# A two-layer graph kernel: first tiles of columns 3 to 6 taken through both hops inside column 1

## The chip, the cores and the metric

The kernel runs on one core of a Trainium2 chip. The metric is the device time of one execution in microseconds (us), the median of several runs. The engines are named as the profile names them: PE is TensorE (PEld its weight loads), DVE is VectorE, ACT is ScalarE, POOL is GpSimd, SP the engine that issues the large loads.

## The reference

The graph has 8192 nodes with 128 features each, and `adj` is a symmetric 8192 x 8192 float32 matrix of zeros and ones (256 MB). Three products with it are computed, each followed by a small projection:

```python
h = maximum(layernorm(x), 0)
x1 = swish((adj @ h) @ W0 + b0)          # first hop
x = x + swish((adj @ x1) @ W0 + b0)      # second hop
h = maximum(layernorm(x), 0)
a_hat = adj + eye;  d = sum(a_hat, axis=1) ** -0.5
out = ((a_hat * d[:, None] * d[None, :]) @ h) @ W1.T + b1   # third hop
x = x + out
```

## The kernel before

**Work and tiles.** The output nodes are split into 16 columns of 512. A tile is 512 source nodes by one column, 1 MB in float32, so that a column has 16 tiles and `adj` has 256. Each tile is loaded once, into a ring of 4 buffers (`ring`, `RING`). DVE or ACT turns it into one byte per element (`mark`, `act_mark`; the tiles in `ACT_MARKED` are ACT's), in a ring of 8 byte tiles (`marks`, `MARK_RING`), and DVE packs four byte tiles at a time to one bit per element (`pack_half`, `pack_again`, `pack_last`), which is kept in `bits` for later. A buffer of `ring` is free for the next load when its tile is marked and, unless the tile is in `LATE`, when ACT has also counted its nonzero elements with a Sign activation (`counted`). SP waits for just that before each load. A tile in `LATE` is loaded again in the third hop and counted there.

**The first hop** multiplies every tile with h: 8 matmuls of 512 columns for each tile, in order of arrival, into `acc_ps`. When column c is done, its sums go through a chain over four engines: ACT `sums_out`, PE `project`, DVE `add_bias` and `scale_z`, ACT `sigmoid`, DVE `gate`, ACT `high_part`, DVE `low_part`. The last sets `node_ready`: the result of column c is then an input of the second hop. `FINISH` and `FINISH_FIRST` give the tile of the next column behind which each of these steps stands.

**The second hop, as far as it can be done while tiles arrive.** Tile i of column c needs the first hop's result of column i alone. In column c the tiles up to c - 2 are therefore multiplied a second time at once (`early`, into `early_ps`), and for columns 0 to 2 the missing blocks are unpacked from `bits` (`kept_unpack`) and multiplied a little later (`kept_block`, 12 blocks of two matmuls in a column, 8 the first time). `AHEAD` puts tiles of late columns into the order of the earlier ones: behind tiles 7 and 11 of columns 2 and 3, two columns at a time, the first two tiles of each. Such a tile is taken through both hops on the spot (`unit_ahead`), the partial sums are moved out by ACT (`save_x` after the first hop's 16 matmuls, `save_y` after the second's), and POOL adds them back when the column's own turn comes. The tiles' own places are then holes.

**After the last load**, `PIECES` goes through the rest of the second hop and the whole third hop from `bits`, unpacked by DVE into `ring` in pieces of two units (`unpack`), four pieces ahead of PE at most. In the third hop each column is a step k of 64 blocks (128 matmuls) and one projection; in each, SP loads `LATE_STEP` tiles of `LATE` again, and ACT (Sign) and DVE (`late_check`) count them. All engines run their instructions in the order of the program, so that whatever waits holds up what is behind it on its engine.

## Time and profile before

| | us |
|---|---|
| runs | 1430.45, 1431.73, 1432.16 (median 1431.73) |
| profiled execution, its own time | 1429.92 |
| its span, first to last instruction | 1428.1 |
| PE busy | 1382.2 (97%) |
| DVE busy | 1055.0 (74%) |
| ACT busy | 685.2 (48%) |

A timeline row gives the start and the length of an instruction in us, engine, line, what it writes and reads, and in brackets how long the engine had been idle before it and who ended that. The length of a matmul in such a row (0.38) overlaps with the next one's; the distance between two starts is what one costs. The tiles are numbered below by the order in which they are loaded, from 0: "load 16" is tile 0 of column 1.

### The profile page before, as it was taken

The numbers are of one execution on the slowest core, as the hardware profiler recorded it, in microseconds if no ns is written. First come the engines' busy times: TensorE is split into PE (matmuls) and PEld (weight loads), VectorE is DVE, ScalarE is ACT, GpSimd is POOL, SyncE is SP. The second block draws the span as 40 slices with busy tenths as digits, with TensorE's granted clock in tenths as the row PEclk, the third lists the DMA queues.
The fourth block names the chain that finished last, engine by engine and source line by source line (L and its number), as shares of the span: only waits on it lengthen the run. The fifth ranks groups of instructions, "written<-read, shape, count | busy, mean of one in ns | idle before, by whom it ended". The sixth has DMA issues, their size and how long they took to land.

```text
span 1428.1 us, 18554 instructions
## 1 busy us (share of the span) xinstructions
PE 1382.2 (97%) x6600; PEld 650.5 (46%) x6600; DVE 1055.0 (74%) x2327; ACT 685.2 (48%) x798; POOL 62.1 (4%) x47
## 2 busy tenths in 40 slices
PE   3889999999999999999999999999999999999997
PEld 1334444444444444444444454454444444444443
DVE  7878777899999988977694767786766566657630
ACT  6785738888878676567540122222322322332200
POOL 1100000000100100000000011100000000000000
PEclk9999999999999999999999999999999999999999
DMA  9999999999999988798730112112453435343300
GB/s 395 409 421 394 406 405 385 413 421 414 400 392 395 367 346 323 308 370 320 315 150 30 52 45 68 66 67 89 192 195 144 191 134 198 141 190 136 139 23 17
DMA packets 58420, 352.23 MB, mean 247 GB/s; under 512 B 6481, under 2 KB 6866, under 8 KB 18386
## 3 DMA queue, kind: packets, MB, share of 16 engines
q1 hardware_dynamic: 51696, 339.11, 59.6%
q10 hardware_dynamic: 6626, 11.87, 2.2%
q8 instruction: 55, 0.90, 0.3%
q14 instruction: 43, 0.35, 0.1%
HBM read 339.15 MB, written 11.80 MB: 246 GB/s over the span
## 4 chain that ended last, share of the span: by engine, by line
PE 87%; DMA 6%; ACT 3%; DVE 2%; issue 1%; SPq 0%; POOL 0%; ACTq 0%; DVEq 0%
PE acc_ps L740 21%; PE acc_ps L741 21%; PE acc_ps L675 11%; PE acc_ps L676 11%; DMA ring<-adj 6%; PE early_ps L606 5%; PE early_ps L604 5%; PE z_ps L587 3%; PE kept_ps L614 2%; PE kept_ps L615 2%; ACT marks L816 1%; PE acc_ps L631 1%; PE early_ps L645 1%; PE acc_ps L632 1%; PE early_ps L644 1%
## 5 line engine op out<-in xcount | busy, mean ns | idle before, releaser
L899 ACT ACTIVATE unused<-ring 128x2048 uint8<-128x2048 uint32 x204 | 389.4, 1909 | 70.5 <-DMA ring<-adj 61.5
L675 PE MATMUL acc_ps<-marks,node_a 128*128 128x512 fp8e4 x960 | 368.0, 383 | 35.3 <-DVE node_a L1057 24.6
L741 PE MATMUL acc_ps<-ring,node_a 128*128 128x512 fp8e4 x1024 | 388.1, 379 | 0.0
L740 PE MATMUL acc_ps<-ring,node_a 128*128 128x512 fp8e4 x1024 | 388.1, 379 | 0.0
L676 PE MATMUL acc_ps<-marks,node_a 128*128 128x512 fp8e4 x960 | 368.0, 383 | 0.0
L1065 DVE TENSOR_SCALAR marks<-ring 128x2048 uint8<-128x2048 f32 x230 | 285.6, 1242 | 81.1 <-DMA ring<-adj 40.0
L1354 DVE TENSOR_SCALAR_CACHE_REDUCE count_a<-marks 128x2048 uint8<-128x2048 f32 x52 | 118.7, 2284 | 113.9 <-DMA marks<-adj 112.5
L437 DVE TENSOR_SCALAR ring<-bits 128x256 uint32<-128x256 uint32 (+1 forms) x784 | 158.7, 276 | 40.7 <-PE acc_ps L741 40.5
L675 PEld LDWEIGHTS acc_ps<-marks,node_a 128*128 128x128 f16 x960 | 94.7, 99 | 156.8 <-issue 48.5
L741 PE MATMUL acc_ps<-ring,node_b 128*128 128x512 fp8e5 x416 | 157.7, 379 | 0.0
L740 PE MATMUL acc_ps<-ring,node_b 128*128 128x512 fp8e4 x416 | 157.7, 379 | 0.0
L740 PEld LDWEIGHTS acc_ps<-ring,node_a 128*128 128x128 f16 x1024 | 100.3, 98 | 118.8
L741 PEld LDWEIGHTS acc_ps<-ring,node_a 128*128 128x128 f16 x1024 | 100.2, 98 | 119.0
L676 PEld LDWEIGHTS acc_ps<-marks,node_a 128*128 128x128 f16 x960 | 94.7, 99 | 113.2 <-issue 4.6
L947 ACT ACTIVATE nT<-acc_ps 128x512 f32<-128x512 f32 x16 | 9.6, 597 | 264.4 <-PE acc_ps L741 264.4
L604 PE MATMUL early_ps<-marks,node_b 128*128 128x512 fp8e4 x352 | 133.4, 379 | 0.0
L606 PE MATMUL early_ps<-marks,node_b 128*128 128x512 fp8e5 x352 | 133.4, 379 | 0.0
L955 ACT ACTIVATE unused<-marks 128x2048 uint8<-128x2048 uint32 x52 | 99.2, 1908 | 56.5 <-DMA marks<-adj 54.9
L1073 DVE SCALAR_TENSOR_TENSOR xnew<-marks 128x1024 uint32<-128x1024 uint32 (+1 forms) x68 | 81.8, 1203 | 0.4 <-ACT marks L816 0.4
L932 ACT ACTIVATE y<-xnew,nmr,rstd 128x128 f32<-128x128 f32 x64 | 26.4, 483 | 104.3 <-DVE nmr L1347 104.3
L1157 DVE TENSOR_TENSOR zb<-z_ps,b_sb 128x512 f32<-128x512 f32 x32 | 22.1, 690 | 62.9 <-PE z_ps L587 62.7
L614 PE MATMUL kept_ps<-kept_marks,node_b 128*128 128x512 fp8e4 x164 | 62.1, 379 | 1.7 <-issue 1.7
(137 smaller groups left out, 1205.8 us busy)
## 6 DMA issues: line engine op xcount, KB each, us to landing
ring<-adj SPq DMA_DIRECT2D x256, 1024.0 KB, 7.8
marks<-adj SPq DMA_DIRECT2D x52, 1024.0 KB, 5.4
node_b<-x SPq DMA_DIRECT2D x4, 1024.0 KB, 11.0
xch<-x SPq DMA_DIRECT2D x16, 256.0 KB, 2.8
xn_scratch<-xnew ACTq DMA_DIRECT2D x16, 256.0 KB, 2.0
xch<-xn_scratch SPq DMA_DIRECT2D x16, 256.0 KB, 2.8
out<-xnew ACTq DMA_DIRECT2D x16, 256.0 KB, 2.0
part_scratch<-stage ACTq DMA_DIRECT2D x13, 256.0 KB, 7.0
```

The source lines that it names most:

```text
L437: return nc.vector.tensor_scalar(dst, src, abs(MARK_BIT - BIT[k]), MARK_WORD, shift, ALU.bitwise_and)
L604: nc.tensor.matmul(into[:, :], hi_of(node_b16, j), byte.bitcast(E4), start=(j == (2 * TB if c in AHEAD_COLUMNS else 0)), stop=False)
L606: last = nc.tensor.matmul(into[:, :], lo_of(node_b16, j), byte.bitcast(E5), start=False, stop=(c > 2 and j == (c - 1) * CB - 1))
L614: nc.tensor.matmul(kept_ps[n][:, :], hi_of(node_b16, j), byte.bitcast(E4), start=(j == 0), stop=False)
L675: nc.tensor.matmul(acc_ps[c % 2][:, :], hi_of(node_a16, j), byte, start=(j == opens * TB), stop=False)
L676: last = nc.tensor.matmul(acc_ps[c % 2][:, :], lo_of(node_a16, j), byte, start=False, stop=(j == NB - 1))
L740: nc.tensor.matmul(into[:, :], hi_of(node, j), byte.bitcast(E4), start=opens, stop=False)
L741: last = nc.tensor.matmul(into[:, :], lo_of(node, j), byte.bitcast(low), start=False, stop=closes)
L899: nc.scalar.activation(unused[:, :], loaded_slot(g).bitcast(U32), ACT.Sign, accum_out=nz_count[:, g:g + 1]).then_inc(counted, 1)
L955: nc.scalar.activation(unused[:, :], late_slot(e).bitcast(U32), ACT.Sign, accum_out=nz_count[:, LATE[e]:LATE[e] + 1]).then_inc(late_counte ...
L1065: nc.vector.tensor_scalar(mark_tile(e.at), loaded_slot(e.g), 1.0, MARK, ALU.is_equal, ALU.mult).then_inc(marked, 1)
L1354: nc.vector.tensor_scalar(late_junk, late_slot(e), 1.0, None, ALU.is_equal, ALU.add, accum_out=late_one[:, e:e + 1]).then_inc(late_ones, 1)
```

## The change

The change moves the first use of the second hop from column 2 into column 1.

- `AHEAD` gets a fifth group: behind tile 3 of column 1 stand the first tiles of columns 3, 4, 5 and 6, one of each, through both hops (`take_ahead`). The groups of two columns move to tiles 3, 7 and 11 of column 2 and tile 7 of column 3. In all, 20 tiles are taken ahead in place of 16, and 12 columns in place of 8 have saved sums that POOL adds.
- Column 0's chain is pressed into the first tiles of column 1: sums out and projection behind tile 0, bias behind 2, sigmoid behind 3, gate and high part with the first tile taken ahead, low part with the second. Column 1's chain stands the same way in column 2.
- Column 0's kept blocks (8, with `kept_unpack` behind tile 7) move from column 2 to tiles 8 to 15 of column 1.
- ACT marks every fourth tile up to column 8, where it did so up to column 4: 42 tiles in place of 26. Three more tiles of columns 1 and 2 are not counted on arrival (`UNSIGNED`). `LATE` grows from 52 to 75 tiles, `LATE_STEP` from 4 to 6, and the buffers for them from 2 to 6 (four lie in `node_b`, which the third hop does not read).
- The table for Sigmoid is loaded in column 0, and `feature_scales` runs before the third packing.

```diff
-ACT_MARKED = [1, 3, 4, 7, 9, 11] + [TC + i for i in range(1, TC, 2)] + [g for g in range(2 * TC, 5 * TC) if g % 4 == 3]
-AHEAD = {2 * TC + 7: (13, 14), 2 * TC + 11: (11, 12), 3 * TC + 7: (9, 10), 3 * TC + 11: (7, 8)}
+ACT_MARKED = [1, 3, 4, 7, 9, 11] + [TC + i for i in range(1, TC, 2)] + [g for g in range(2 * TC, 9 * TC) if g % 4 == 3]
+AHEAD = {TC + 3: (3, 4, 5, 6), 2 * TC + 3: (13, 14), 2 * TC + 7: (11, 12), 2 * TC + 11: (9, 10), 3 * TC + 7: (7, 8)}
+AHEAD_TILES = {c: 4 // len(ahead) for ahead in AHEAD.values() for c in ahead}
+UNSIGNED = [TC, TC + 2, 2 * TC + 1]
-LATE_STEP = 4
+LATE_STEP = 6
+LATE_SLOTS = 6
+FINISH_ZERO = {"sums out": 0, "project": 0, "bias": 2, "scale": 2, "sigmoid": 3, "gate": TC, "high": TC, "low": TC + 1}
...
                     if e.ahead:
-                        first, second = AHEAD[OWN_BEFORE[e.at]]
-                        if (c, i) == (second, 1):
-                            save_x(first)
-                            save_y(first)
+                        ahead = AHEAD[OWN_BEFORE[e.at]]
+                        which = ahead.index(c)
+                        if which > 0 and i == AHEAD_TILES[c] - 1:
+                            save_x(ahead[which - 1])
+                            if which < 3:
+                                save_y(ahead[which - 1])
+                        if finish_at("high", e):
+                            high_part(now_of(e) - 1)
...
                     if g - 1 in AHEAD:
-                        save_x(AHEAD[g - 1][1])
+                        if len(AHEAD[g - 1]) == 4:
+                            save_y(AHEAD[g - 1][2])
+                        else:
+                            save_x(AHEAD[g - 1][1])
                     if g - 2 in AHEAD:
-                        save_y(AHEAD[g - 2][1])
+                        if len(AHEAD[g - 2]) == 4:
+                            save_x(AHEAD[g - 2][3])
+                        save_y(AHEAD[g - 2][-1])
...
-                    if e >= 2:
-                        sp.wait_ge(late_counted, e - 1)
-                        sp.wait_ge(late_ones, e - 1)
-                    sp.dma_start(late_slot(e), adj_t[LATE[e], :, :]).then_inc(late_in[e % 2], 16)
+                    if e >= LATE_SLOTS:
+                        sp.wait_ge(late_counted, e - LATE_SLOTS + 1)
+                        sp.wait_ge(late_ones, e - LATE_SLOTS + 1)
+                    sp.dma_start(late_slot(e), adj_t[LATE[e], :, :]).then_inc(late_in[e % LATE_SLOTS], 16)
```

On ACT, in column 1 before: from the count of tile 2 (the Sign that writes `unused`) on, a mark and a count in turn, with column 0's sums (`nT<-acc0_ps`) between them.

```order
L899 ACTIVATE unused,nz_count<-ring 128x2048 [waits counted,tile_in2]
L849 ACTIVATE nT<-acc0_ps 128x512 [waits tile_mm]
L816 ACTIVATE marks<-ring 128x2048 [waits pack4_ready,tile_mm,tile_in3]
L899 ACTIVATE unused,nz_count<-ring 128x2048 [waits counted,tile_in0]
L816 ACTIVATE marks<-ring 128x2048 [waits pack4_ready,tile_mm,tile_in1]
L899 ACTIVATE unused,nz_count<-ring 128x2048 [waits counted,tile_in2]
L816 ACTIVATE marks<-ring 128x2048 [waits pack4_ready,tile_mm,tile_in3]
L899 ACTIVATE unused,nz_count<-ring 128x2048 [waits counted,tile_in0]
L865 ACT_TABLE_LOAD
L865 ACTIVATE sig<-zb 128x512 [waits zb_ready]
```

The same stretch of ACT in the changed kernel, from column 0's sums on: `bits<-acc0_ps` is `save_x` and `node_b<-early_ps` is `save_y`, of columns 3, 4, 5 and 6 in turn.

```order
L895 ACTIVATE nT<-acc0_ps 128x512 [waits tile_mm]
L862 ACTIVATE marks<-ring 128x2048 [waits pack4_ready,tile_mm,tile_in1]
L862 ACTIVATE marks<-ring 128x2048 [waits pack4_ready,tile_mm,tile_in3]
L911 ACTIVATE sig<-zb 128x512 [waits zb_ready]
L915 ACTIVATE node_b<-y 128x512 [waits yn_ready]
L866 ACTIVATE bits<-acc0_ps 128x512 [waits x_done]
L871 ACTIVATE node_b<-early_ps,alpha 128x2x256 [waits alpha_ready,tile_mm]
L866 ACTIVATE bits<-acc0_ps 128x512 [waits x_done]
L871 ACTIVATE node_b<-early_ps,alpha 128x2x256 [waits alpha_ready,tile_mm]
L866 ACTIVATE bits<-acc0_ps 128x512 [waits x_done]
L951 ACTIVATE unused,nz_count<-ring 128x2048 [waits tile_in0]
L871 ACTIVATE node_b<-early_ps,alpha 128x2x256 [waits alpha_ready,tile_mm]
```

Before, marks and counts take turns. Now the sigmoid, the high part and five of the eight saves stand ahead of the first count, that of tile 4 of column 1 (load 24), and no mark stands among them.

On DVE, in column 1 before, from column 0's bias (`zb<-z_ps`, behind tile 7) to its gate (`y<-y,sig`, behind tile 10); the low part, `node_b<-node_b,y`, comes ten rows behind the gate.

```order
L1157 TENSOR_TENSOR zb<-z_ps,b_sb 128x512 [waits z_done,count_step]
L1108 TENSOR_TENSOR count_a<-count_a,count_b 128x2048
L1065 TENSOR_SCALAR marks<-ring 128x2048 [waits tile_mm,pack4_ready,tile_in0,count_step]
L1073 SCALAR_TENSOR_TENSOR xnew<-marks 128x1024 [waits act_marked,marked]
L1162 TENSOR_TENSOR y<-zb,s_row 128x512 [waits zb_ready]
L1080 SCALAR_TENSOR_TENSOR xch<-xnew 128x512 [waits pack4_ready]
L1190 COPY alpha<-misc_ps 128x1 [waits s_col_done]
L1192 TENSOR_SCALAR alpha<-alpha 128x1 [waits alpha_copied]
L1108 TENSOR_TENSOR count_a<-count_a 128x1024
L1065 TENSOR_SCALAR marks<-ring 128x2048 [waits tile_mm,pack4_ready,tile_in2,count_step]
L1092 SCALAR_TENSOR_TENSOR bits<-xch 128x256 [waits pack2_ready]
L1167 SCALAR_TENSOR_TENSOR y<-y,sig 128x512 [waits sig_ready,zs_ready]
```

On DVE in the changed kernel, from the same bias, behind tile 2, to the low part; the two marks are of the first tiles of columns 3 and 4 (loads 20 and 21).

```order
L1239 TENSOR_TENSOR zb<-z_ps,b_sb 128x512 [waits z_done]
L1244 TENSOR_TENSOR y<-zb,s_row 128x512 [waits zb_ready]
L1183 TENSOR_SCALAR count_a<-bits 128x1024 [waits bits_ready]
L1272 COPY alpha<-misc_ps 128x1 [waits s_col_done,count_step]
L1274 TENSOR_SCALAR alpha<-alpha 128x1 [waits alpha_copied]
L1188 TENSOR_TENSOR count_b<-bits,count_a 128x2048
L1122 TENSOR_SCALAR marks<-ring 128x2048 [waits tile_mm,pack4_ready,tile_in0,count_step]
L1130 SCALAR_TENSOR_TENSOR xnew<-marks 128x1024 [waits act_marked,marked]
L1249 SCALAR_TENSOR_TENSOR y<-y,sig 128x512 [waits sig_ready,zs_ready]
L1122 TENSOR_SCALAR marks<-ring 128x2048 [waits pack4_ready,tile_mm,tile_in1]
L1137 SCALAR_TENSOR_TENSOR xch<-xnew 128x512 [waits pack4_ready]
L1253 SCALAR_TENSOR_TENSOR node_b<-node_b,y 128x512 [waits hi_ready]
```

The gate and the low part each stand behind one mark of a tile taken ahead, and the low part closes the chain two marks behind the bias, where it stood seven tiles behind it.

On DVE in the third hop before, the first column's late checks (`late_one<-marks`), the bias for the output, and the next piece's unpacking (`ring<-bits`).

```order
L1354 TENSOR_SCALAR count_a,late_one<-marks 128x2048 [waits late_in0]
L1354 TENSOR_SCALAR count_a,late_one<-marks 128x2048 [waits late_ones,late_in1]
L1354 TENSOR_SCALAR count_a,late_one<-marks 128x2048 [waits late_ones,late_in0]
L1354 TENSOR_SCALAR count_a,late_one<-marks 128x2048 [waits late_ones,late_in1]
L1362 TENSOR_TENSOR xch<-xch,b_sb 128x512 [waits xch_in0,w1_in]
L437 TENSOR_SCALAR ring<-bits 128x2x128 [waits slot_used]
L437 TENSOR_SCALAR ring<-bits 128x2x128 x7
```

The same place in the changed kernel: two more checks stand ahead of that piece.

```order
L1437 TENSOR_SCALAR count_a,late_one<-marks 128x2048 [waits late_in0]
L1437 TENSOR_SCALAR count_a,late_one<-marks 128x2048 [waits late_ones,late_in1]
L1437 TENSOR_SCALAR count_a,late_one<-node_b 128x2048 [waits late_ones,late_in2]
L1437 TENSOR_SCALAR count_a,late_one<-node_b 128x2048 [waits late_ones,late_in3]
L1437 TENSOR_SCALAR count_a,late_one<-node_b 128x2048 [waits late_ones,late_in4]
L1437 TENSOR_SCALAR count_a,late_one<-node_b 128x2048 [waits late_ones,late_in5]
L1445 TENSOR_TENSOR xch<-xch,b_sb 128x512 [waits xch_in0,w1_in]
L482 TENSOR_SCALAR ring<-bits 128x2x128 [waits slot_used]
L482 TENSOR_SCALAR ring<-bits 128x2x128 x7
```

## Rows read from the trace of the kernel before

**Rows 1.** Five stretches: busy PE, PEld, DVE, ACT, POOL; granted clock, DMA share, GB/s.

```profile
57.00:80.00 23.00, 20.27 (x98) 9.54 (x97) 19.56 (x29) 17.69 (x16) 0.00 (x0) 1.00 0.98 401
80.00:100.00 20.00, 16.20 (x67) 6.38 (x66) 14.52 (x25) 17.41 (x16) 0.00 (x0) 0.91 1.01 420
84.00:87.00 3.00, 3.00 (x9) 1.06 (x7) 2.29 (x5) 3.00 (x4) 0.00 (x0) 0.50 1.01 415
100.00:115.00 15.00, 12.24 (x64) 5.94 (x63) 12.81 (x19) 12.34 (x12) 0.00 (x0) 1.00 1.02 422
115.00:263.00 148.00, 148.00 (x702) 68.25 (x701) 112.77 (x141) 91.30 (x96) 0.00 (x0) 1.00 1.00 398
```

**Rows 2.** Timeline of PE: first matmuls of loads 16, 25 and 113.

```profile
61.78 0.38 PE L675 MATMUL acc_ps<-marks,node_a 128*128 128x512 fp8e4 x1 [0.71 <-DVE marks L1065]
...
83.52 0.48 PE L675 MATMUL acc_ps<-marks,node_a 128*128 128x512 fp8e4 x1 [2.57 <-ACT marks L816]
...
313.18 0.38 PE L675 MATMUL acc_ps<-marks,node_a 128*128 128x512 fp8e4 x1
313.40 0.38 PE L676 MATMUL acc_ps<-marks,node_a 128*128 128x512 fp8e4 x1
```

**Rows 3.** Timeline of DVE in column 1: count step, packing, mark of load 28, low part.

```profile
65.73 1.23 DVE L1108 TENSOR_TENSOR count_b<-bits,count_a 128x2048 uint16<-128x2048 uint16 x1
...
68.13 1.22 DVE L1073 SCALAR_TENSOR_TENSOR xnew<-marks 128x1024 uint32<-128x1024 uint32 x1
...
87.63 1.23 DVE L1065 TENSOR_SCALAR marks<-ring 128x2048 uint8<-128x2048 f32 x1 [1.28 <-DMA ring<-adj]
...
94.08 0.69 DVE L1171 SCALAR_TENSOR_TENSOR node_b<-node_b,y 128x512 f16<-128x512 f16 x1
```

**Rows 4.** Timeline of ACT in column 1: Sign of load 16, the high part.

```profile
56.24 1.91 ACT L899 ACTIVATE unused<-ring 128x2048 uint8<-128x2048 uint32 x1 [4.20 <-DMA ring<-adj]
...
86.98 0.61 ACT L869 ACTIVATE node_b<-y 128x512 f16<-128x512 f32 x1
```

**Rows 5.** DMA of the ring, start to 120 us: from issue to landing.

```profile
DMA to landing us min/median/max: 4.8/8.0/19.5
```

**Rows 6.** Timeline of ACT at the last group taken ahead, loads 72 to 75.

```profile
211.23 0.60 ACT L820 ACTIVATE bits<-acc_ps 128x512 f32<-128x512 f32 x1 [8.05 <-PE acc_ps L632]
214.69 0.69 ACT L825 ACTIVATE node_b<-early_ps,alpha 128x512 f32<-128x512 f32 x1 [2.86 <-PE early_ps L645]
215.27 1.90 ACT L899 ACTIVATE unused<-ring 128x2048 uint8<-128x2048 uint32 x1
...
224.07 1.90 ACT L816 ACTIVATE marks<-ring 128x2048 uint8<-128x2048 f32 x1
```

**Rows 7.** Timeline of DVE: marks of loads 78, 80, 112 and 113.

```profile
217.98 1.23 DVE L1065 TENSOR_SCALAR marks<-ring 128x2048 uint8<-128x2048 f32 x1 [0.38 <-DVE count_a L1108]
...
224.95 1.23 DVE L1065 TENSOR_SCALAR marks<-ring 128x2048 uint8<-128x2048 f32 x1 [3.88 <-DMA ring<-adj]
...
307.94 1.23 DVE L1065 TENSOR_SCALAR marks<-ring 128x2048 uint8<-128x2048 f32 x1 [0.33 <-DMA ring<-adj]
...
310.43 1.23 DVE L1065 TENSOR_SCALAR marks<-ring 128x2048 uint8<-128x2048 f32 x1
```

**Rows 8.** Timeline of DVE in the third hop: first and fourth check, next unpacking.

```profile
996.53 2.29 DVE L1354 TENSOR_SCALAR_CACHE_REDUCE count_a<-marks 128x2048 uint8<-128x2048 f32 x1 [9.73 <-DMA marks<-adj]
...
1006.22 2.29 DVE L1354 TENSOR_SCALAR_CACHE_REDUCE count_a<-marks 128x2048 uint8<-128x2048 f32 x1 [0.18 <-DMA marks<-adj]
...
1009.03 1.70 DVE L437 TENSOR_SCALAR ring<-bits 128x256 uint32<-128x256 uint32 x8
```

**Rows 9.** Timeline of ACT, at the end of the third hop's second column.

```profile
1019.16 0.60 ACT L947 ACTIVATE nT<-acc_ps 128x512 f32<-128x512 f32 x1 [10.94 <-PE acc_ps L741]
```

**Rows 10.** Timeline of POOL at the end of column 0.

```profile
51.97 1.10 POOL L544 TENSOR_SCALAR node_a<-node_b 128x1024 f16<-128x1024 f32 x1 [1.06 <-ACT node_b L836]
```

**Rows 11.** Timeline of DVE at the same time: a mark.

```profile
52.09 2.07 DVE L1065 TENSOR_SCALAR marks<-ring 128x2048 uint8<-128x2048 f32 x1
```

More of the change, by code:

```diff
@@ L82, in __init__ @@
         self.c, self.i = g // TC, g % TC
-        self.hole = not ahead and self.c in AHEAD_COLUMNS and self.i < 2
+        self.hole = not ahead and self.i < AHEAD_TILES.get(self.c, 0)
 def entries():
@@ L90, in entries @@
         for c in AHEAD.get(g, ()):
-            for i in range(2):
+            for i in range(AHEAD_TILES[c]):
                 order.append(Entry(len(order), c * TC + i, True))
@@ L103, in units_of @@
 def units_of(r):
[L105 removed]
+    return range(1 if ORDER[4 * r + 1].hole else 0, 2)
 def groups_upto(c):
@@ L132, with now_of, kept_unpack_after @@
 AHEAD_IN = {c: g // TC for g, pair in AHEAD.items() for c in pair}
-SAVED_BY = {now + 1: 2 * sum(g < (now + 1) * TC for g in AHEAD) for now in sorted({g // TC for g in AHEAD})}
+SAVED_BY = {now + 1: sum(len(AHEAD[g]) for g in AHEAD if g < (now + 1) * TC) for now in sorted({g // TC for g in AHEAD})}
 FINISH = {"sums out": 2, "project": 4, "bias": 7, "scale": 8, "sigmoid": 8, "gate": 10, "high": 11, "low": 14}
-FINISH_FIRST = {"sums out": 1, "project": 3, "bias": 5, "scale": 6, "sigmoid": 5, "gate": 7, "high": 7, "low": None}
+FINISH_ZERO = {"sums out": 0, "project": 0, "bias": 2, "scale": 2, "sigmoid": 3, "gate": TC, "high": TC, "low": TC + 1}
+FINISH_FIRST = {"sums out": 0, "project": 0, "bias": 2, "scale": 2, "sigmoid": 3, "gate": TC, "high": TC, "low": TC + 1}
+def now_of(e):
+    return AHEAD_IN[e.c] if e.ahead else e.c
 def finish_at(what, e):
+    now = now_of(e)
     if e.ahead:
-        return what == "low" and e.at == OWN[2 * TC + 7] + 2
-    return e.c >= 1 and e.i == (FINISH_FIRST if e.c == 2 else FINISH)[what]
-KEPT_UNPACK_AFTER = 3
+        place = TC + e.at - OWN[min(g for g in AHEAD if g // TC == now)] - 1
+    else:
+        place = e.i
+    return now >= 1 and place == {1: FINISH_ZERO, 2: FINISH_FIRST}.get(now, FINISH)[what]
+KEPT_SOURCE = {1: 0}
+KEPT_SOURCE.update((c, c - 2) for c in range(3, NC))
+FIRST_KEPT_AFTER = (8, 9, 10, 11, 12, 13, 14, 15)
+def kept_unpack_after(c):
+    return 7 if c == 1 else 3
 COUNT_AFTER = (2, 3, 5, 6, 7, 9, 11, 11, 11, 13, 15)
@@ L618, in _, with take_ahead @@
             pe.wait_ge(w_in, 32)
-            def unit_ahead(now, pair, c, at):
+            def take_ahead(now, before, c, at):
                 into = acc_ps[(now + 1) % 2]
+                tiles = range(AHEAD_TILES[c])
                 pe.wait_ge(nT_ready, now)
-                if pair > 0:
-                    pe.wait_ge(x_saved, pair)
-                for i in range(2):
+                if before > 0:
+                    pe.wait_ge(x_saved, before)
+                for i in tiles:
                     pe.wait_ge(marked, marked_upto(at + i))
@@ L631, in unit_ahead @@
                         nc.tensor.matmul(into[:, :], hi_of(node_a16, j), byte, start=(j == 0), stop=False)
-                        last = nc.tensor.matmul(into[:, :], lo_of(node_a16, j), byte, start=False, stop=(j == 2 * TB - 1))
+                        last = nc.tensor.matmul(into[:, :], lo_of(node_a16, j), byte, start=False, stop=(j == len(tiles) * TB - 1))
                 last.then_inc(x_done, 1)
-                if pair > 0:
-                    pe.wait_ge(y_saved, pair)
+                if before > 0:
+                    pe.wait_ge(y_saved, before)
                 if now >= KEPT:
                     pe.wait_ge(early_ready, now - KEPT + 1)
-                for i in range(2):
+                for i in tiles:
                     pe.wait_ge(node_ready, i + 1)
@@ L1248, in _ @@
                     r, place = e.at // GT, e.at % GT
-                    if g not in ACT_MARKED and not e.hole:
+                    if g not in ACT_MARKED and not e.hole and g > TC:
                         mark(e)
```

119 lines of the change are left out of this document (76 added, 43 removed).

## The prediction

> **What bounds the kernel now.** I read three views: busy time by stretches, the timelines of PE, DVE and ACT side by side, and the marks that start the moment a tile lands. The stretches come first. From 115 us to 263 us PE is busy throughout. Before that it is not: it is busy 20.27 of 23.00 us from 57 to 80, 16.20 of 20.00 from 80 to 100 and 12.24 of 15.00 from 100 to 115 [rows 1]. These are 9.3 us without work, and from 84 to 87 its granted clock is 0.50 on top, the lower of its two levels (1.2 of 2.4 GHz), after a wait of 2.57 us for a mark [rows 1, 2]; 3 us at that level cost 1.5. Two starts of matmuls stand 0.22 us apart (0.2156 over many), so that a tile costs 8 x 0.2156 = 1.73 us of PE in one hop [rows 2]. Two loads land 2.49 us apart: the marks of loads 112 and 113 start so, as they land [rows 7]. In columns 1 and 2 PE has nearly only the first hop to do and starves; later it has both, and has a backlog.
>
> So there are about 11 us to win at most, and the change goes for them. But the DMA's share is 0.98 to 1.02 in all of these stretches [rows 1]: two streams are full here, not one. The reader should therefore also ask when the loads come. Load 16 lands at 56.24, load 113 at 310.43 [rows 4, 7]. 97 loads at 2.485 would take 241.0 us, and they take 254.2: the stream stood still for 13.2 us. The largest such pause is behind the last group taken ahead: the marks of loads 78 and 80 are 6.97 us apart, 2.0 more than two loads take [rows 7]. The cause is on ACT: it waits 8.05 us and 2.86 us for PE's ahead sums and can count the tiles behind them only then, and marks load 79 at 224.07 [rows 6]; the ring's four buffers come free late.
>
> **How much of it can come back.** What can PE save? PE's work is the same in both kernels, only its place differs. By load 113 (tile 1 of column 6) both have done exactly the same: counted in the code, both have multiplied every tile of columns 0 to 5, the same kept blocks, and the same tiles of columns 6 to 14 ahead. From there on the order is the same. So the changed kernel can start load 113 only as soon as that tile is marked. Before, it landed and was marked at 310.43, for 1.23 us, and PE began it at 313.18 [rows 2, 7]; with 0.15 us from mark to matmul PE was 1.4 us behind the data. The gain is 1.4 us plus what the stream of loads gains. That is the sum's first term, whatever happens in column 1.
>
> **The stream in the changed kernel, step by step.** PE is free for load 16 a little before 61.78 [rows 2], and its mark is now made ahead of the feature scales, so it starts at about 60.9. Loads 16 to 19, the projection (0.9) and a small matmul take 8.1 us, to 69.0. DVE has by then, behind the mark of load 18 (done at 64.6 as before): packing, bias, scaling, two count steps (0.69 and 1.23) and the constants, then the mark of load 20, done at 69.8: PE waits 0.9. It multiplies load 20 in the first hop, to 71.6, and wants the node data of column 0. DVE still has a packing (1.22), the gate, the mark of load 21, a packing and the low part (0.69) [rows 3], to 74.0; ACT's high part (0.61) lies beside them [rows 4]. PE waits 2.4. Seven more half units of 1.73 end at 86.3. So 3.3 us of waiting are left there, and the rest of column 1 has 3.5 us of kept blocks more than before: PE itself would run about 7 us ahead of the old kernel by column 2.
>
> ACT pays for it. The count of load 24 stands behind the third save of first-hop sums, which PE finishes only at 81.0; the count (1.91 [rows 4], and 0.2 to read it) ends at 83.8. Before, it stood right behind the landing, four loads ahead of load 28, which landed and was marked at 87.63 [rows 3]: at 77.7. Load 28 can be issued only then, and the shortest issue to landing is 4.8 us [rows 5]: it lands at 88.7 at best, I take 89.2, where it was there by 87.6. The mark of load 25, two saves and the count of load 26 follow one another on ACT, to 89.6, and the loads 29 and 30 wait for these in turn. A count (2.1) and a mark (1.90) [rows 6] take 2.0 us per tile against 2.49, so ACT catches up, by load 35, and the stream is then about 2.2 us late (2.0 at the least, 4.3 if each load of the queue starts from empty). This is the price of the group in column 1.
>
> Against it stand the later groups. Before, the pauses behind the four groups come to half of the 13.2 us, some 6.7, and 2.0 of that is the one of rows 7, where PE is furthest behind. The new order has three of them in column 2 and only one in column 3, with PE less far behind at it; by the same waits I get 3.8 in all, 2.9 less. The marks that ACT takes over in columns 5 and 6 free DVE for 1.23 us each; pauses of 0.2 us by load 113. The other pauses (stores of partial sums, about 5.5 us) stay. Net: 2.2 - 2.9 - 0.2 = 0.9 less, I take 0.7. **First term: 1.4 + 0.7 = 2.1 us faster.** Its bounds: a stream later by the whole 4.3 and none of the 2.9 back gives 1.4 - 4.3 = 2.9 slower; no pause in column 1 and 2.9 back gives 1.4 + 3.1 = 4.5 faster.
>
> POOL adds saved sums for four more columns. In the trace a DVE mark takes 2.07 us where POOL runs at the same time, and 1.23 elsewhere [rows 7, 10, 11]. The Trainium skill (SBUF — State Buffer, section "Who interferes with whom") holds that DVE and GpSimd share one pair of ports and that the later one is blocked for the whole of the other's instruction; the trace agrees with a blocked mark. By that rule an add that meets the mark of load 113 would make the first term 0.85 smaller. I leave it out of the sum: the adds are two in a column of 16 tiles.
>
> **The third hop.** Late checks go from 52 to 75, six in a step. A step lasts 28.5 us and DVE's six checks 14.2, with four pieces to unpack (1.70 each) and 3 us of the rest: 24, it fits, and six buffers let the loads run ahead. But the first step has little room. There the first check starts at 996.53, as the first late tile lands, the fourth at 1006.22, and the next piece is unpacked from 1009.03 to 1010.73 [rows 8]. PE ends that column at about 1019.0, when ACT takes its sums at 1019.16 [rows 9], and a piece is 32 x 0.2156 = 6.9 us: it begins the piece at 1012.05, 1.3 us after it is unpacked. In the changed kernel the sixth tile lands 5 x 2.485 behind the first, at 1008.95; its check ends at 1011.2, 0.6 of bias and 1.7 of unpacking follow, to 1013.5. **Second term: PE waits 1.45 us, slower.** Bounds: nothing, if two more checks overlap better, to 4.7 - 1.3 = 3.4, if both are added whole. In the later steps the piece is ready 5 us or more ahead. The larger compare at the end has two steps behind it; the table load and the feature scales lie beside waits.
>
> **Sum.** 1.45 - 2.1 = 0.65 us faster. The profiled execution had 1429.92 (span 1428.1 and 1.8 around it), 1.8 below the median of 1431.73; taken off the median, 1431.1. A change under 0.2%, 2.9 us, can't be told from none.
>
> **Rivals.**
> - The stream is held up less: ACT's count in column 1 comes in time, or the groups cost little. For it speaks that four buffers and a queue cover about 4 us; against it that the count is 4 us late by the waits above. 4.5 faster, less 1.45 or nothing: 3.1 to 4.5 faster, 1427.2 to 1428.6; if all pauses of the groups went, 6.7 + 1.4, 1423.7. Chance 0.25.
> - Slower: ACT's saves hold the loads. It is decided by whether load 28 and its three followers are issued more than 4 us late. Then the stream is 4.3 late, nothing comes back in column 2, whose three groups now stand close together, and the first term is 2.9 slower; with 1.45, 1436.1. Another stall of PE of some 2.5 us may lower the clock again, as at 84 us [rows 1], and cost 1.5. Chance 0.18.
> - The change moves PE's waits and no more: the chain of column 0 costs what its second hop fills, the stream stays as it was. First term 1.4, second 1.45: 1431.7. Chance 0.15.
> - The forecast, 2.1 and 1.45 with an error of 2 on the stream: 1429 to 1433.5. Chance 0.42.
>
> **Numbers.** The range goes from the first rival's middle to short of the slow one's end: 1427.3 to 1435.0. Faster by over 0.2% takes the first rival and little of the forecast, 0.27; slower 0.17; the rest, 0.56, within it.
>
> **What the new profile would show.** PE waits once for the low part in column 1, some 2.4 us, and hardly from 80 to 115 us; ACT's count of load 24 starts at 81 to 82 and not at 78; load 28 lands 1 to 3 us late; load 113 is marked at about 309.7 and begun 0.15 us after, so that PE waits for marks of columns 4 to 6 where it did not; in the third hop PE waits once, at 1.4 us, in its second column. The forecast is wrong if load 113 lands more than 3 us earlier or 2 later than 310.4, or if the later steps of the third hop wait for DVE.

## The result and the profile after

| | before | after |
|---|---|---|
| median of 20 runs, us | 1430.68 | 1427.13 |
| lowest and highest | 1428.42, 1432.67 | 1425.09, 1432.06 |
| profiled execution, span | 1428.1 | 1427.0 |

The ratio is 0.998, with a 95% interval of 0.9973 to 0.9987: 2.9 us faster (1.9 to 3.9), and 3.5 by the two medians. On the 1431.73 of the forecast the ratio gives 1428.9: inside the range, and 2.2 us under the forecast of 1431.1. The profiled execution of after took 1428.83, which is 1.7 above its median; that of before was 0.8 below its own. Single executions of one kernel spread widely, over 4.3 us before and 7.0 after, and this matters below.

The same five stretches in after, with the columns of [rows 1]:

```profile
57.00:80.00 23.00, 20.24 (x99) 9.58 (x98) 21.55 (x32) 7.89 (x9) 0.00 (x0) 1.00 0.99 402
80.00:100.00 20.00, 19.84 (x93) 8.83 (x92) 12.75 (x21) 17.12 (x17) 0.00 (x0) 1.00 0.89 353
84.00:87.00 3.00, 3.00 (x16) 1.34 (x14) 2.86 (x9) 3.00 (x5) 0.00 (x0) 1.00 0.61 240
100.00:115.00 15.00, 12.88 (x59) 5.46 (x58) 9.32 (x12) 10.31 (x9) 0.00 (x0) 1.00 1.01 423
115.00:263.00 148.00, 144.91 (x689) 66.19 (x686) 120.05 (x151) 92.46 (x95) 4.83 (x3) 1.00 1.00 404
```

Three things are to be seen. PE is busy for 19.84 of the 20 us from 80 to 100, where it was for 16.20. The DMA's share, full before, falls to 0.89 there and to 0.61 from 84 to 87: the loads now pause. And from 115 to 263 PE, busy throughout before, stands idle for 3.1 us. What was won in front is paid behind.

PE's timeline shows what is left in column 1 (the first matmul of load 20, the first with node data) and, as the last row, the piece of the third hop:

```profile
69.83 0.38 PE L677 MATMUL acc_ps<-marks,node_a 128*128 128x512 fp8e4 x1 [0.53 <-issue]
73.95 0.38 PE L690 MATMUL early_ps<-marks,node_b 128*128 128x512 fp8e4 x1 [2.23 <-DVE node_b L1253]
...
1013.98 0.38 PE L786 MATMUL acc_ps<-ring,node_a 128*128 128x512 fp8e4 x1 [1.25 <-DVE ring L482]
```

By the starts of matmuls, less the 0.2156 that one costs, the three waits are 0.69, 2.40 and 1.41 us; the forecast had 0.9, 2.4 and 1.45. ACT's timeline behind the group, third save and count of load 24:

```profile
81.06 0.60 ACT L866 ACTIVATE bits<-acc_ps 128x512 f32<-128x512 f32 x1 [1.04 <-PE acc_ps L678]
81.55 1.90 ACT L951 ACTIVATE unused<-ring 128x2048 uint8<-128x2048 uint32 x1
83.35 0.19 ACT L951 ACTIVATION_READ_ACCUMULATOR unused<-ring 128x1 f32 x1
83.45 0.68 ACT L871 ACTIVATE node_b<-early_ps,alpha 128x512 f32<-128x512 f32 x1
84.02 1.91 ACT L862 ACTIVATE marks<-ring 128x2048 uint8<-128x2048 f32 x1
```

The load that waits for this count, load 28, is issued at 83.63 and lands at 88.50.

Then load 113, where the forecast settled its first term. Before, its mark started at 310.43 and PE began it at 313.18 [rows 2, 7]. After, DVE's timeline (packing, mark of 113), ACT's (mark of load 112) and PE's:

```profile
310.69 1.23 DVE L1130 SCALAR_TENSOR_TENSOR xnew<-marks 128x1024 uint32<-128x1024 uint32 x1 [1.34 <-ACT marks L862]
311.83 1.22 DVE L1122 TENSOR_SCALAR marks<-ring 128x2048 uint8<-128x2048 f32 x1
...
308.68 1.91 ACT L862 ACTIVATE marks<-ring 128x2048 uint8<-128x2048 f32 x1 [0.48 <-DMA ring<-adj]
...
313.20 0.38 PE L721 MATMUL acc_ps<-marks,node_a 128*128 128x512 fp8e4 x1 [0.36 <-DVE marks L1122]
```

PE begins load 113 at 313.20, as late as before. Behind it come two waits that the kernel before did not have, 0.47 us for a mark at 352.64 and the 1.41 of the third hop:

```profile
352.64 0.38 PE L721 MATMUL acc_ps<-marks,node_a 128*128 128x512 fp8e4 x1 [0.31 <-DVE marks L1122]
```

So the last column's output is written by DVE at 1422.37, where it was at 1420.45. Yet the span is 1.1 us *shorter*. The rows that say so are the last rows of DVE in before and in after:

```profile
1420.45 1.13 DVE L1375 SCALAR_TENSOR_TENSOR xnew<-z_ps,dinv,xch 128x128 f32<-128x128 f32 x4 [24.72 <-PE z_ps L587]
```

```profile
1422.37 1.13 DVE L1458 SCALAR_TENSOR_TENSOR xnew<-z_ps,dinv,xch 128x128 f32<-128x128 f32 x4 [24.72 <-PE z_ps L632]
```

From these starts to the end of the span it is 7.65 us before and 4.63 after. The work of the profiled execution got 1.9 us longer; the 3.0 us of the end more than paid it. No view shows the end, since branches and waits are not counted as busy; the trace's records of single instructions do. On ACT, in us:

```text
kernel  store of last output issued / has landed / jump over the general path / last DRAIN / span
before  1421.61   1424.48   1424.53   1427.82   1428.1     jump to DRAIN 3.28
after   1423.53   1426.21   1426.26   1426.72   1427.0     jump to DRAIN 0.45
```

ACT waits for the store, then jumps over the code of the general path (`eng.Else()`) to its last instruction. That takes 3.28 us in one kernel and 0.45 in the other, and the code on both sides of the jump is the same.

### The profile page after: what moved, and what is told of

It reads as the page before. It is cut to its first block and busy times, and to the rows that moved or that the text cites. A ratio compares the mean times of both kernels' runs of the same rounds, so it can differ in the third digit from the quotient of the medians.

```text
span 1427.0 us, 18691 instructions
## 1 busy us (share of the span) xinstructions
PE 1382.0 (97%) x6600; PEld 649.3 (45%) x6600; DVE 1103.0 (77%) x2372; ACT 720.8 (51%) x823; POOL 73.0 (5%) x55
## 5 line engine op out<-in xcount | busy, mean ns | idle before, releaser
L721 PE MATMUL acc_ps<-marks,node_a 128*128 128x512 fp8e4 x944 | 360.8, 382 | 33.1 <-DVE node_a L1114 24.7
L951 ACT ACTIVATE unused<-ring 128x2048 uint8<-128x2048 uint32 x181 | 345.5, 1909 | 57.4 <-DMA ring<-adj 49.8
L722 PE MATMUL acc_ps<-marks,node_a 128*128 128x512 fp8e4 x944 | 360.8, 382 | 0.0
L1122 DVE TENSOR_SCALAR marks<-ring 128x2048 uint8<-128x2048 f32 x214 | 265.5, 1241 | 68.9 <-DMA ring<-adj 34.5
L721 PEld LDWEIGHTS acc_ps<-marks,node_a 128*128 128x128 f16 x944 | 92.9, 98 | 154.3 <-issue 47.8
L722 PEld LDWEIGHTS acc_ps<-marks,node_a 128*128 128x128 f16 x944 | 92.8, 98 | 110.0 <-issue 3.5
L649 PE MATMUL early_ps<-marks,node_b 128*128 128x512 fp8e4 x336 | 127.3, 379 | 0.0
L651 PE MATMUL early_ps<-marks,node_b 128*128 128x512 fp8e5 x336 | 127.3, 379 | 0.0
L1437 DVE TENSOR_SCALAR_CACHE_REDUCE count_a<-node_b 128x2048 uint8<-128x2048 f32 x49 | 112.0, 2286 | 10.8 <-DMA node_b<-adj 5.8
L1012 ACT ACTIVATE unused<-node_b 128x2048 uint8<-128x2048 uint32 x49 | 93.6, 1910 | 9.7 <-DMA node_b<-adj 4.6
L1130 DVE SCALAR_TENSOR_TENSOR xnew<-marks 128x1024 uint32<-128x1024 uint32 x69 | 83.1, 1204 | 13.5 <-ACT marks L862 13.5
L862 ACT ACTIVATE marks<-ring 128x2048 uint8<-128x2048 f32 x42 | 80.2, 1909 | 18.4 <-DMA ring<-adj 18.4
```

The source lines that it names most:

```text
L649: nc.tensor.matmul(into[:, :], hi_of(node_b16, j), byte.bitcast(E4), start=(j == AHEAD_TILES.get(c, 0) * TB), stop=False)
L651: last = nc.tensor.matmul(into[:, :], lo_of(node_b16, j), byte.bitcast(E5), start=False, stop=(c > 2 and j == (c - 1) * CB - 1))
L721: nc.tensor.matmul(acc_ps[c % 2][:, :], hi_of(node_a16, j), byte, start=(j == opens * TB), stop=False)
L722: last = nc.tensor.matmul(acc_ps[c % 2][:, :], lo_of(node_a16, j), byte, start=False, stop=(j == NB - 1))
L951: nc.scalar.activation(unused[:, :], loaded_slot(g).bitcast(U32), ACT.Sign, accum_out=nz_count[:, g:g + 1]).then_inc(counted, 1)
L1012: nc.scalar.activation(unused[:, :], late_slot(e).bitcast(U32), ACT.Sign, accum_out=nz_count[:, LATE[e]:LATE[e] + 1]).then_inc(late_counte ...
```

## The experiments

Twelve kernels. The times are medians; each ratio is to the kernel before on the same chip. e1 to e4 ran on one chip, e5 to e8 on a second, e9 to e12 on a third, where the medians of the kernel before were 1430.48, 1430.60 and 1431.15. The ratio takes in all executions and is not the quotient of the two medians, which for e3 would be 0.9966. An interval reaches 1.3 to 2.0 us either way; where two kernels lie closer than that, only their traces can tell them apart. "ACT's code filled up" means instructions that only raise a semaphore, in the last column but one of the third hop, so that ACT's program has as many instructions as after's; for e5 to e12 this keeps the end alike.

| kernel | us | ratio (95%) |
|---|---|---|
| e1 before, 45 on ACT | 1427.98 | 0.9977 (0.9968 to 0.9987) |
| e2 after, 83 on ACT | 1429.97 | 0.9994 (0.9985 to 1.0003) |
| e3 after, first late step of four | 1425.66 | 0.9958 (0.9945 to 0.9972) |
| e4 after, load 24 not counted | 1428.06 | 0.9976 (0.9965 to 0.9987) |
| e5 e3, ACT marks to column 4 | 1430.47 | 1.0001 (0.9992 to 1.001) |
| e6 e3, no group in column 1 | 1428.78 | 0.998 (0.9971 to 0.9989) |
| e7 e3, ACT free in column 1 | 1422.57 | 0.9946 (0.9933 to 0.996) |
| e8 e5 and e7 | 1427.93 | 0.9981 (0.9972 to 0.999) |
| e9 before, ACT marks to column 8 | 1428.58 | 0.9982 (0.9973 to 0.9991) |
| e10 e6, 128 on PE | 1427.72 | 0.997 (0.9958 to 0.9983) |
| e11 e7, load 112 marked by DVE | 1423.58 | 0.9946 (0.9933 to 0.996) |
| e12 e1, 128 on PE | 1435.52 | 1.0026 (1.0014 to 1.0038) |

### e1 and e2: the end alone

e1 on the kernel before; e2 has 83 in place of 45 and stands on the changed kernel.

```diff
                 if n > 0:
                     store_out(n - 1)
+                if n == NC - 2:
+                    for _ in range(45):
+                        act.sem_inc(act_step, 1)
```

> The kernel before with 45 instructions that only raise a semaphore on ACT, in the last column but one of the third hop, where ACT idles 28 us a column. ACT then has as many instructions as in the changed kernel, 45 more than before. Then this kernel, which changes nothing but that place, ends 2.8 us sooner: 0.998 of the time before, 1427.9 us, with ACT's last DRAIN under 1 us behind its last wait. Theory B: the whole gain is in the work (stalls of columns 1 and 2) and the end of one profile is chance: 1430.7 us, ratio 1.000, DRAIN still some 3 us behind.

Both came out as theory A had them: 1427.98 for 1427.9, and 1429.97 for 1429.9. The records on ACT:

```text
e1      1422.49   1425.31   1425.37   1425.82   1426.1     jump to DRAIN 0.45
e2      1424.02   1426.70   1426.76   1429.99   1430.3     jump to DRAIN 3.23
```

Every later kernel with after's count of instructions on ACT jumps in 0.45 too. So 2.8 of the 3.5 us between the medians is the place of a jump. It also gives two pairs in which the ends are alike. By the medians after is 0.85 faster than e1, and e2 0.5 faster than before. By the ratios after is 0.4 slower than e1 (0.998 against 0.9977), and e2 0.9 faster than before, with an interval from 2.1 faster to 0.4 slower. What the change does to the work can't be told from nothing here; the forecast had 0.65 us.

### e3: the wait in the third hop

```diff
+def late_of(n):
+    first = max(0, n * LATE_STEP - 2)
+    return range(first, min((n + 1) * LATE_STEP - 2, len(LATE)))
...
-range(n * LATE_STEP, min((n + 1) * LATE_STEP, len(LATE)))
+late_of(n)
```

> The changed kernel with four late tiles instead of six in the first column of the third hop (six in each later one; all 75 still counted). Theory A (the second term of the prediction): PE's wait of 1.41 us at the last piece of the second column is gone, since VectorE unpacks it 2.4 us sooner, and the time falls by as much: 1425.7 us, 0.9965 of before. Rival: another wait of the third hop takes its place (the next slack is 3.4 us), and the time stays at 1427.1.

1425.66, as expected: 1.47 below after by the medians, 3.1 by the ratios. The traces say it more surely: with six tiles the wait is there (1.41 us in after, 1.26 in e2, 1.42 in e4), with four PE has no wait at that place, and the piece is unpacked from 1004.61 to 1006.31, 5.1 us before PE begins it. No other wait takes its place: every later piece is ready 8.6 us or more ahead. The second term stands, and is a loss that two tiles in another step avoid.

### e4 and e7: who holds the load stream in column 1

```diff
-UNSIGNED = [TC, TC + 2, 2 * TC + 1]
+UNSIGNED = [TC, TC + 2, TC + 4, 2 * TC + 1]
```

> The changed kernel with the count of tile 4 of column 1 taken off ACT and put among the late tiles (76 of them). Theory A (the prediction's term of the held stream): ACT's count of this load starts at 81.7 us behind the third save and releases load 28 at 83.6; without it the slot is free at the end of the last multiplication or of the mark, load 28 lands 1 to 2 us sooner, every load up to load 113 as well, and the time falls by 1 to 2.2 us against the changed kernel: 1425.0 to 1426.1 us, 0.996 to 0.997 of before. Rival: the stream is bound by the DMA engines between the loads and catches up, or other counts of ACT hold it again at the next slots: 1427.1 us, 0.998.

1428.06, no gain: the rival was right. Load 28 is issued 5.3 us sooner (78.38), and load 29 now waits, until 86.72, for the mark of load 25, which ACT can make only behind its saves. ACT's timeline in e4:

```profile
84.21 0.69 ACT L871 ACTIVATE node_b<-early_ps,alpha 128x512 f32<-128x512 f32 x1 [1.13 <-PE early_ps L691]
84.79 1.90 ACT L862 ACTIVATE marks<-ring 128x2048 uint8<-128x2048 f32 x1
```

Load 35 lands at 109.70, and in e3, without this edit, at 109.69 (at 108.90 in after, where the granted clock did not fall, see below). The hold is ACT's queue and not one instruction in it. So e7, on e3, takes all four tiles from ACT:

```diff
-ACT_MARKED = ... + [TC + i for i in range(1, TC, 2)] + ...
+ACT_MARKED = ... + [TC + i for i in (1, 3, 9, 11, 13, 15)] + ...
-UNSIGNED = [TC, TC + 2, 2 * TC + 1]
+UNSIGNED = [TC, TC + 2, TC + 4, TC + 5, TC + 6, TC + 7, 2 * TC + 1]
```

> The kernel of e3 with ACT free for the saves: tiles 4 to 7 of column 1 are neither counted nor marked by ACT (VectorE marks all four, their counts go among the late tiles), ACT's code filled up. Theory A: the load stream was held at load 28 by ACT's count behind the third save, and in e4, where only that count was taken away, at load 29 by ACT's mark of load 25 behind the last saves; with none of the four on ACT load 28 lands at 87, load 35 by 107.5 instead of 109.7, and the time falls by 2.2 us (the hold) to 1423.5; if the stream stands still elsewhere for part of it, by 1. Rival B: VectorE, with two more marks, is late for loads 24 to 30 and TensorE waits for it: 1425.7 to 1427.

1422.57: 3.1 below e3 where 2.2 was expected, and 4.6 below after. Against e3 the ratios give 1.7 and the intervals overlap, but in the traces PE begins load 113 3.8 us sooner; against after the intervals lie apart. DMA and PE are full where both had gaps; the same stretches in e7:

```profile
80.00:100.00 20.00, 20.00 (x94) 9.09 (x93) 17.65 (x26) 12.40 (x12) 0.00 (x0) 1.00 1.01 422
100.00:115.00 15.00, 15.00 (x78) 7.41 (x77) 9.24 (x14) 10.43 (x9) 0.00 (x0) 1.00 1.01 422
```

DVE, with two more marks (17.65 us busy for 12.75), starts that of load 28 1.3 us behind its landing, but PE waits for none of them. The landings read from the traces, and how long the stream stood still (what lies over 2.485 us a load), in us:

```text
kernel   load 16   load 35   load 113   stood still 16-35   35-113   PE begins load 113
before    56.22    104.94    310.40          1.5            11.6        313.18
e1        56.37    105.11    310.89          1.5            12.0        313.27
e9        56.06    104.93    309.38          1.7            10.6        312.36
after     56.40    108.90    311.13          5.3             8.4        313.20
e2        56.20    110.98    311.87          7.6             7.1        313.93
e3        56.20    109.69    309.78          6.3             6.3        311.85
e4        56.24    109.70    310.83          6.2             7.3        312.89
e5        56.14    107.46    310.34          4.1             9.0        313.02
e7        56.17    105.14    306.01          1.8             7.0        308.08
e12       57.06    106.61    318.86          2.3            18.4        321.58
```

The price of the group is the column "16-35": 2.6 to 6.1 us over before in the five traces that have it with ACT's four tiles in place (after, e2 to e5), and 0.3 in e7. It was lower where the granted clock stayed full behind PE's wait of 2.40 us (after and e5: 3.8 and 2.6) than where it fell (e2, e3, e4: 6.1, 4.8, 4.7). What comes back is the next column.

### e5, e8 and e9: ACT's marks to column 8

```diff
-ACT_MARKED = ... + [g for g in range(2 * TC, 9 * TC) if g % 4 == 3]
+ACT_MARKED = ... + [g for g in range(2 * TC, 5 * TC) if g % 4 == 3]
```

> The kernel of e3 (four late tiles in the first column of the third hop) with ACT's marks only to column 4, as before the change, and ACT's code filled up to the same count of instructions, so that its end falls alike. Theory A: ACT marks tile 15 of column 5 (load 112) in 1.91 us where VectorE takes 1.23, VectorE's packing waits for it, and its mark of load 113 stands behind: 0.69 us late, on TensorE's path. Without ACT's marks of columns 5 to 8 the mark begins as load 113 lands: 1425.0 us, 0.7 below e3. Rival B: ACT's marks relieve VectorE in columns 5 and 6 so that marks are on time there, and without them the time rises by 0.5 to 1.5 us over e3, to 1426.2 to 1427.2.

1430.47: 4.8 slower than e3 (3.3 by the spans of the two profiled executions). Neither theory had this; A is wrong in sign, B too small by more than half. The waits of PE for marks, in e3 and then in e5 (sum, times, longest), behind them one tile of e5 on DVE's timeline and one wait of PE in e5 that is not for a mark:

```profile
PE acc_ps L727 <- DVE marks L1128: 3.1, 5, 0.9
PE acc_ps L727 <- ACT marks L868: 2.2, 2, 1.2
```

```profile
PE acc_ps L728 <- DVE marks L1132: 5.6, 9, 1.3
PE acc_ps L728 <- ACT marks L869: 3.5, 4, 1.2
```

```profile
290.05 1.63 DVE L1198 TENSOR_TENSOR count_a<-count_a,count_b 128x2048 uint16<-128x2048 uint16 x1
291.71 1.23 DVE L1132 TENSOR_SCALAR marks<-ring 128x2048 uint8<-128x2048 f32 x1
```

```profile
318.42 0.39 PE L728 MATMUL acc_ps<-marks,node_a 128*128 128x512 fp8e4 x1 [0.92 <-issue]
```

The mark at 291.71 is load 105's, which landed at 288.15: DVE is 3.6 us behind the data, where it was 0.6 behind in e3. PE stands at almost every tile from 304 to 318, and again at 354 and 392, 5.8 us in all against 1.3 in e3. Of these 5.8 us 4.7 are waits for marks; 1.1 is the wait for "issue" at 318.42, 2.5 us behind the start of a fetch of PE's code at 315.9 (the next section is about such fetches), and no lack of marks. Before, at the same tile, DVE was 1.6 behind, and PE had slack.

> The edits of e5 and e7 together on e3. Theory A: both terms add, 0.7 and 2.2 us below e3: 1422.8 us, 0.9945 of before. Rival B: one of them is used up by the other, since TensorE's wait for load 113 has a slack of its own: 1423.5 to 1425.

1427.93. With e7's edit the lack costs 5.4, a wait for "issue" of 1.4 at 314.9 included; neither theory had it, for the same reason. On the kernel before the marks do nothing that these runs can tell:

> The kernel before with the other half of the change alone: ACT's marks to column 8, six late buffers and late steps of six (four in the first), no group in column 1 and the last steps of column 0 in their old places; ACT's code filled up to the changed kernel's count, so it compares with e1 (1428.0 us). Theory A: ACT's marks pay only where the group has brought TensorE and the stream ahead of VectorE (e5 against e3: 4.8 us); before, TensorE waited for data and not for VectorE's marks in columns 4 to 7, so they are worth nothing alone: 1427.5 to 1428.3 us, equal to e1, and TensorE begins load 113 at about 313. Rival B: VectorE held the stream in the kernel before too (its marks of column 6 stood 1 to 3 us behind the landings), and the marks alone gain 1.5 to 3 us: 1425 to 1426.5.

1428.58, level with e1 (ratios 0.9982 and 0.9977): theory A. Marks alone are worth nothing, the group without them (e5) is 2.5 slower than e1, and both together with e3's edit are 2.3 faster. The two halves of the change pay only together, as far as kernels compared over three chips show it.

### e6, e10 and e12: the group alone, and PE's code

e6 takes the group out of `AHEAD` and puts gate and high part of column 0 behind tile 4 of column 1, the low part behind tile 5. e10 and e12 add the second edit below ahead of PE's first wait, where it has no data for 24 us:

```diff
-AHEAD = {TC + 3: (3, 4, 5, 6), 2 * TC + 3: ...
+AHEAD = {2 * TC + 3: ...
```

```diff
+            for _ in range(128):
+                pe.sem_inc(pe_step, 1)
```

> The kernel of e3 without the four early tiles behind tile 3 of column 1 (columns 3 to 6 then take their first tiles in their own order); column 0's last steps are still early, ACT's code filled up to the same count. Theory A (the prediction's first term, 2.1 us, comes from the group): TensorE waits for loads in column 1 as before and the time rises by about 2 us over e3, to 1427.7. Rival B: the load stream alone sets when load 113 is begun, and without the group's saves on ACT the stream is not held at load 28 (some 2 to 3 us): the time is equal to e3's or up to 1.5 us below it, 1424.2 to 1425.7.

> The kernel of e6 (no group in column 1, 1428.8 us) with 128 instructions on TensorE that only raise a semaphore, ahead of its first wait, in the 24 us in which it has no data. Its code is fetched in blocks of 16384 bytes (256 instructions); this moves every boundary by half a block. In e6's trace TensorE stands for 2.55 us at 108.2 and for 2.52 at 189.2, waiting for nothing but issue, each just ahead of such a fetch's arrival. Theory A: these stalls are the fetch; they go or move, and if both go the time falls by what the stream of loads doesn't hold back, 0.5 to 3 us: 1426 to 1428.3. Rival B: they stand at a place of the program (a queue or a semaphore) and stay where they are: 1428.8 us.

> The kernel of e1 (that of before with ACT's code filled up, 1428.0 us) with the same 128 instructions on TensorE. Its stall of 1.86 us at 111.2 (1.59 in e1's trace), waiting for issue, stands at a fetch of TensorE's code too. Theory A: it moves away or goes; TensorE waits for loads anyway behind it, so that the time stays within 0.5 us of 1428.0 unless a boundary falls on a place without slack, where it would rise by up to 2.5. Rival B: the stall stays at 111 us and the time at 1428.0.

e6 is at 1428.78, 3.1 above e3: theory A, but not cleanly, since its trace has two stalls of PE that wait for nothing shown. In e10 both are gone, one of 2.9 us stands at another place, and the time is 1427.72. The group is worth 3.1 us by e6 and 2.1 by e10, stalls in both that e3 does not have included, so these are upper bounds rather than its price. In e12, e1's stall at 111 us has gone, two others stand elsewhere, and the time is 7.5 *higher* (7.0 by the ratios); I had put the worst at 2.5. The waits of PE in e6, e10 and e12:

```profile
PE misc_ps L647 <- issue: 2.5, 1, 2.5
PE acc_ps L729 <- issue: 2.4, 1, 2.4
```

```profile
PE acc_ps L731 <- issue: 2.9, 1, 2.9
```

```profile
PE acc_ps L679 <- issue: 4.4, 1, 4.4
PE kept_ps L616 <- issue: 3.0, 1, 3.0
```

All stand at a fetch of PE's code: the fetches on queue 8 begin at 108.6 and 189.6 in e6, 97.2 in e10, 101.5 and 181.9 in e12, and PE goes on 2.4 to 2.6 us behind each. Behind both of e12's the granted clock fell: from 100 to 115 it is 0.77 of full speed. It fell behind both of e6's and e10's one too; e6 from 111 to 114:

```profile
111.00:114.00 3.00, 3.00 (x8) 1.11 (x9) 2.41 (x4) 0.63 (x1) 0.00 (x0) 0.54 1.00 418
```

The stalls lie where the loads fill the DMA. That alone does not make one: before, six such fetches begin between 115 and 263 us at a DMA share of 1.00, and PE is busy throughout [rows 1]. What else it takes stays open. In e12 the stream stood still 18.4 us instead of 12.0 (table above), and the pauses that e1 lacks follow the stalls: 4.5 us for 0.7 from load 35 to 50, 4.6 for 0.2 from load 65 to 74. That PE frees byte tiles late there, and marks and loads wait in turn, is my reading; I did not follow it load by load. The change moves such fetches as well: PE stands 1.59 us at 113 in e1 and 0.94 at 107.6 in after, and no run takes this apart from the rest of the change.

### e11: load 112 back to DVE

```diff
-ACT_MARKED = ... + [g for g in range(2 * TC, 9 * TC) if g % 4 == 3]
+ACT_MARKED = ... + [g for g in range(2 * TC, 9 * TC) if g % 4 == 3 and g != 5 * TC + 15]
```

> The kernel of e7 (1422.6 us) with load 112 (tile 15 of column 5) marked by VectorE and not by ACT. Theory A: the mark takes 1.23 us instead of 1.91, the packing behind it starts as much sooner, and the mark of load 113 stands no more 0.70 us behind its landing: TensorE's waits of 0.67 for load 112 and 0.74 for load 113 shrink by 0.7 in all and the time falls to 1421.9. Rival B: VectorE has one mark of 1.23 us more at that place, so load 113 is as late as before: 1422.6.

1423.58, with the ratio of e7 to the digit (0.9946): rival B. DVE's timeline in e11, from the mark of load 112:

```profile
303.50 1.23 DVE L1132 TENSOR_SCALAR marks<-ring 128x2048 uint8<-128x2048 f32 x1 [0.26 <-DMA ring<-adj]
304.64 0.28 DVE L1198 TENSOR_TENSOR count_a<-count_a 128x256 uint16<-128x256 uint16 x1
304.96 0.69 DVE L1227 TENSOR_SCALAR_CACHE_REDUCE count<-count_a 128x512 f16<-128x512 uint8 x1
305.57 0.08 DVE L1227 DVE_READ_ACCUMULATOR count<-count_a 128x1 f32 x1
305.57 1.22 DVE L1140 SCALAR_TENSOR_TENSOR xnew<-marks 128x1024 uint32<-128x1024 uint32 x1
306.71 1.22 DVE L1132 TENSOR_SCALAR marks<-ring 128x2048 uint8<-128x2048 f32 x1
```

The count's last steps, done in e7 while DVE waited for ACT, now stand in front of the packing, and load 113's mark starts at 306.71 as in e7.

## Why the prediction was right, and where not

- **What it left out.** The sum ran from load 16 to the last matmul of the third hop and took what lies behind as unchanged. That was the step that failed: the end got 2.8 us shorter (e1, e2). It is no effect of the group, the marks or the late tiles, only of 45 more instructions on ACT. Without it the change is within 0.2% of before, as forecast. That the sum for the work came out near is luck in part: the price of the group, what the later groups give back and the slack were all mis-sized, and the errors nearly cancel.
- **Second term, 1.45 slower.** Right: 1.41 in the trace, 1.26 and 1.42 in e2 and e4.
- **The path through column 1.** Right to 0.3 us: waits of 0.69 and 2.40 for 0.9 and 2.4, load 24 begun at 86.04 for 86.3, ACT's count at 81.55, load 28 landed at 88.50 for 89.2. That the clock would not fall behind the 2.4 us wait held in after's trace and in those of e5, e7, e8 and e11; in e2 to e4, whose code is the same there, it fell (row below), saves and counts were 1.5 us later, and load 28 landed at 89.8 to 89.9 in e2 and e3. The forecast had this as part of its slow rival. Of the 9.3 us that it counted as PE without work before, 1.86 at 113.3 are a wait for "issue" behind a fetch begun at 110.7, and none for data.
- **Price of the group on the stream, 2.2.** Too small: 2.6 to 6.1 in five traces; the forecast's bounds were 2.0 and 4.3. The forecast let ACT catch up by load 35 at its rate. But each load's issue waits for ACT's work of four loads before, with a drained queue and 4.9 us from issue to landing (83.63 to 88.50; loads 29 and 30 take 5.0), where a load in a full queue lands 2.49 us behind the one before, so that the row "16-35" grows by more than the first delay.
- **What later groups give back, 2.9 and 0.2.** Too small too: 3.4 to 5.5 against the mean of before and e1. The two errors nearly cancel: in after and e2 to e4 load 113 lands at 311.13, 311.87, 309.78 and 310.83, where the forecast had 309.7 and before and e1 have 310.40 and 310.89.
- **The slack of 1.4 at load 113.** 0.3 to 0.7 was there: PE began it 2.78 and 2.38 us behind the landing in before and e1, and 2.07 in all traces of after's order, for its mark starts 0.69 late (the packing behind ACT's mark of load 112). The 0.15 from mark to matmul was right.
- **ACT's marks, 0.2.** The step with the largest error, hidden because the change brings both halves: without them the kernel is 4.8 us slower (e5), of which 1.1 is PE's wait at a fetch. DVE's rate is the third full stream in columns 5 to 7, and the forecast had weighed two.
- **First term as a whole, 2.1.** It is not settled. By the medians (0.5 to 0.85 net, 1.47 lost in the third hop) it is 2.0 to 2.3; by the ratios the net itself runs from 0.4 slower to 0.9 faster. By the profiled executions it is nearly nothing (PE at load 113: 312.97 on the mean of four, 313.22 of two before). The profiled ones of after, e2, e3 and e4 were 0.8 to 2.2 above their medians; why, stays open.
- **The range.** Its lower end, 1427.3, is called the middle of the first rival, which reaches from 1427.2 to 1428.6; it is that rival's fast end.

## What to carry to other kernels

When two engines and the DMA are full in turn, removing PE's waits only moves them: look at which engine stands between a landed tile and the release of its buffer, and clear its whole queue there, not one instruction (e4 against e7). Before believing a gain or loss of some us, look at the time behind the last output and at PE's waits for "issue", and compare kernels filled up to the same number of instructions: 45 on ACT gave 2.8 us, 128 on PE took 7.5. That evens out the end; stalls at fetches in the middle still move with the order of the work. The best version here is e7, 1422.57 us, 0.9946 of before.
